# 64-wide attention on a written table of steps: values' products of a row block in one run, ten buffers for turned probabilities, blocks projected last to first

## The reference

```python
h = _rms(_layernorm(x), ln_w)
q = (h @ wq).reshape(B, S, NHEADS, HEAD_DIM)      # 32 heads of 64
k = (h @ wk).reshape(B, S, KVHEADS, HEAD_DIM)     # 8 key/value heads of 64
v = (h @ wv).reshape(B, S, KVHEADS, HEAD_DIM)
q, k = _rope(q, k)
...
scores = einsum('bqhd,bkhd->bhqk', q, k) / sqrt(HEAD_DIM)
scores = where(causal, scores, -1e30)
attn = softmax(scores, -1)
o = einsum('bhqk,bkhd->bqhd', attn, v)
x = x + o @ wo
```

## Time and profile before

| | |
|---|---|
| median of 3 runs | 2234.08 us (2233.0 to 2237.5) |
| profiled execution, its own time | 2239.73 us |
| its span in the trace | 2237.9 us |
| mean granted TensorE clock | 0.942 of full speed |
| busy share of the span | PE 86%, PEld 54%, DVE 58%, ACT 48%, POOL 40% |
| 64-wide attention, about 842 to 1869 us of the span | PE's slices at 9 tenths or more, clock at full speed in the loop |

### The profile page before, as it was taken

How to read it: one execution, slowest core, us unless ns; L and a number is a source line. 1 busy time by engine, 2 the same in 40 slices (tenths; PEclk the granted TensorE clock), 3 DMA queues, 4 the chain that set the end, 5 groups by cost and what they waited for, 6 DMA issues and landing times.

```text
span 2237.9 us, 37392 instructions
## 1 busy us (share of the span) xinstructions
PE 1923.3 (86%) x11178; PEld 1217.4 (54%) x11178; DVE 1292.1 (58%) x3257; ACT 1080.4 (48%) x2758; POOL 905.6 (40%) x1013
## 2 busy tenths in 40 slices
PE   4979899778787739999999999999999996599995
PEld 2656778533333325666666666666666665455552
DVE  5775453457568466666666666666666665822222
ACT  3324342345455416665566556656665663144442
POOL 4990000022120004444444444444444443468884
PEclk9989899769999979999999999999999997799997
DMA  4000020000000100000000000000000003545556
GB/s 143 1 1 1 9 49 1 1 1 1 1 13 26 39 2 1 1 0 0 0 0 0 0 0 0 0 0 0 0 0 0 0 0 111 206 70 82 84 83 160
DMA packets 61350, 60.76 MB, mean 27 GB/s; under 512 B 13136, under 2 KB 58320, under 8 KB 61264
## 3 DMA queue, kind: packets, MB, share of 16 engines
q0 software_dynamic: 15360, 20.98, 5.9%
q1 hardware_dynamic: 45904, 38.65, 5.4%
HBM read 40.48 MB, written 19.14 MB: 27 GB/s over the span
## 4 chain that ended last, share of the span: by engine, by line
PE 62%; DVE 14%; issue 11%; ACT 7%; POOL 4%; DMA 2%; SPq 0%; ACTq 0%; DVEq 0%; POOLq 0%
PE banks L1804 8%; PE banks L1827 7%; PE banks L1836 6%; PE banks L1815 5%; PE banks L1846 4%; PE banks L1900 3%; PE banks L2024 2%; PE banks L1858 2%; ACT wide_x L1468 2%; PE banks L1875 2%; POOL wdT L751 2%; PE banks L1649 2%; ACT wugT L1482 2%; PE banks L1920 2%; PE banks L1942 1%
## 5 line engine op out<-in xcount | busy, mean ns | idle before, releaser
L1051 DVE TENSOR_REDUCE con<-banks 128x1 f32<-128x256 f32 (+3 forms) x512 | 250.3, 489 | 147.9 <-PE banks L1806 141.1
L1804 PE MATMUL banks<-wide_k,wide_q 128*128 128x512 f32 (+3 forms) x1024 | 300.9, 376 | 0.5 <-ACT wide_k L1419 0.5
L683 POOL TENSOR_TENSOR wugT<-wugT,con 128x512 f32<-128x512 f32 (+1 forms) x256 | 237.6, 934 | 134.8 <-DVE con L1041 134.3
L1804 PEld LDWEIGHTS banks<-wide_k,wide_q 128*128 128x128 f32 x1024 | 159.4, 190 | 132.3 <-issue 87.7
L1827 PE MATMUL banks<-attn 128*64 128x256 f32 x1280 | 208.5, 404 | 0.9 <-ACT attn L1447 0.9
L1846 PE MATMUL banks<-late,xnT 128*128 (+1 forms) x512 | 197.2, 508 | 9.7 <-DVE xn L1067 6.3
L1083 DVE TENSOR_REDUCE con<-banks 128x2 f32<-128x1024 f32 x128 | 154.7, 1214 | 66.5 <-PE banks L1888 65.6
L694 POOL TENSOR_TENSOR attn<-attn 128x320 f32<-128x320 f32 x128 | 111.0, 867 | 200.3 <-DVE attn L1029 200.3
L1432 ACT ACTIVATE wugT<-banks,con 128x512 f32<-128x512 f32 (+1 forms) x256 | 161.1, 632 | 58.4 <-DVE con L1051 55.1
L1836 PE MATMUL banks<-late,attn 128*128 (+1 forms) x512 | 141.7, 399 | 28.1 <-DVE attn L1034 25.9
L2024 PE MATMUL banks<-w,late 128*128 x320 | 158.0, 617 | 2.2 <-ACT late L1561 1.7
(11 more groups left out here) (309 smaller groups left out, 4111.6 us busy)
## 6 DMA issues: line engine op xcount, KB each, us to landing
w<-in_L_ffn_w_dram SPq DMA_DIRECT2D x32, 256.0 KB, 6.4
late<-in_L_ffn_w_dram SPq DMA_DIRECT2D x16, 256.0 KB, 6.4
y_rows<-wqkv1T SPq DMA_DIRECT2D x1, 2176.0 KB, 7.9
x<-in_L_attn_x_dram SPq DMA_DIRECT2D x4, 512.0 KB, 9.1
late<-in_L_ffn_wq_dram SPq DMA_DIRECT2D x2, 1024.0 KB, 7.2
late<-in_L_ffn_wo_dram SPq DMA_DIRECT2D x1, 2048.0 KB, 8.3
h_rows<-wugT SPq DMA_DIRECT2D x1, 2048.0 KB, 7.0
y_rows<-x SPq DMA_DIRECT2D x1, 2048.0 KB, 12.8
```

The lines of the kernel that those rows point to most:

```text
L683: nc.gpsimd.tensor_tensor(p, p, rinv[:, m:m + 1].to_broadcast([P, n]), ALU.mult).then_inc(at.sem["norm"], 1)
L1051: nc.vector.tensor_reduce(negmax[:, a:a + 1], bank[at.sbank(a)][:, 0:P * at.keys(at.row_of(a))], AX, ALU.max, negate=True).then_inc(at.sem ...
L1804: nc.tensor.matmul(sbank[:, 0:keys], wide_q[:, side, i, qcols], wide_k[:, side, w, 0:keys], start=(w == 0), stop=False)
```

## The change

The worked-out list gives way to a written table `WIDE`, which is the steady list; "first", "last" and "drain" are cut from it by round. `n_turned` goes from 5 buffers to 10, one for each pair, and the two waits on the buffer are dropped. Token blocks are projected in the order 3, 2, 1, 0 (`wide_tile`), and the wait before the values copy is now for the last pair that reads that block. The values steps stand in four runs: 0 to 3, 4 to 6, 7 and 8, and 9.

```diff
-            def __init__(self, name, quads, hd, causal, bufs, n_turned, pieces, lag, behind, rest, prepare, late):
+            def __init__(self, name, quads, hd, causal, bufs, n_turned, pieces, behind, schedule):
...
-                rounds = self.stream(4)
...
+                steady = [op for slot in range(self.units) for op in [("scores", 0, slot)] + schedule.get(slot, [])]
...
-        WIDE_NEXT = {0: [("stage", 0)], 4: [("qkv", 0)], 6: [("split", 0), ("qkv", 1)], 7: [("turn_qk", 0)],
...
+        WIDE = {0: [("stage", 1, 0), ("turn", -1, 8)],
+                1: [("project", -1, 1)],
+                2: [("qkv", 1, 0), ("values", -1, 7), ("values", -1, 8)],
+                3: [("turn", -1, 9)],
+                4: [("project", -1, 2), ("split", 1, 0)],
+                5: [("values", -1, 9), ("qkv", 1, 1)],
+                6: [("turn_qk", 1, 0)],
+                7: [("project", -1, 3), ("turn_qk", 1, 1), ("turn", 0, 0), ("split", 1, 1)],
+                8: [("turn", 0, 1), ("qkv", 1, 2)],
+                9: [("turn_qk", 1, 2), ("turn", 0, 2)],
+                10: [("turn_qk", 1, 3), ("turn", 0, 3), ("split", 1, 2), ("qkv", 1, 3)],
+                11: [("turn", 0, 4)],
+                12: [("turn_qk", 1, 4), ("turn", 0, 5), ("values", 0, 0), ("values", 0, 1), ("values", 0, 2), ("values", 0, 3),
+                     ("split", 1, 3)],
+                13: [("turn_qk", 1, 5), ("turn", 0, 6)],
+                14: [("turn_qk", 1, 6), ("project", 0, 0)],
+                15: [("turn_qk", 1, 7), ("values", 0, 4), ("values", 0, 5), ("values", 0, 6), ("turn", 0, 7)]}
+
+        def wide_tile(a):
+
+            return TB - 1 - a
...
-                if t == 0 and reached(n - 1):
-                    v.wait_ge(at.sem["pv"], (n - 1) * len(at.steps))
+                if reached(n - 1):
+                    v.wait_ge(at.sem["pv"], (n - 2) * len(at.steps) + at.last_step(t) + 1)
...
-                        if reached(n0 + a + 1 - at.n_turned):
-                            act.wait_ge(at.sem["pv"], n0 + a + 1 - at.n_turned)
-                        nc.scalar.activation(at.probsT[:, a % at.n_turned, :], bank[PTBANK[1]][:],
+                        nc.scalar.activation(at.probsT[:, a, :], bank[PTBANK[1]][:],
```

More of the change, by code:

```diff
@@ L281, in two_layers @@
         wide_k = operands("wide_k", 4 * S).rearrange("p (u h n) -> p u h n", u=2, h=2)
-        region = Region(second.enter_context(nc.sbuf_tensor("attn2", [P, 5 * S + 512 + 1280 + 4 * S + 512 + DC * B * S], F32)))
-        wide_bufs = shared_buffers(5)
+        region = Region(second.enter_context(nc.sbuf_tensor("attn2", [P, 10 * S + 512 + 1280 + 4 * S + 512 + DC * B * S], F32)))
+        wide_bufs = shared_buffers(10)
         wide_x = operands("wide_x", 2 * (R64 + 2) * P).rearrange("p (u n) -> p u n", u=2)
@@ L318, in __init__ @@
                 self.steps = [(q, k) for q, (r, _g) in enumerate(quads) for k in range(self.keys(r))]
+                assert n_turned == len(self.steps)
                 self.sem = {n: sem(f"{name}_{n}") for n in self.names}
                 self.turns = TB * pieces
-                rounds = self.stream(4)
-                assert rounds[1] == rounds[2] and len(rounds) == 5
-                self.windows = {"first": [op for op in rounds[0] if (op[0], op[2]) not in sum(late.values(), [])],
-                                "steady": rounds[2], "last": [op for op in rounds[3] if op[1] <= 0], "drain": rounds[4]}
+                steady = [op for slot in range(self.units) for op in [("scores", 0, slot)] + schedule.get(slot, [])]
+                self.windows = {"first": [op for op in steady if op[1] >= 0], "steady": steady,
+                                "last": [op for op in steady if op[1] <= 0], "drain": [op for op in steady if op[1] < 0]}
                 uses = lambda w: sum(op[0] in ("qkv", "project") for op in self.windows[w])
@@ L351, in y_before @@
                 return TB if window == "first" else it * self.y_uses["per_round"] + self.y_uses["steady"]
[L353 to L390, removed]
-                    slot += 1
-                return out
         RING = 16
@@ L414, in projected_at @@
             return (n, rest // 2) if rest in (0, 2) and 0 <= n < B else None
-        WIDE_NEXT = {0: [("stage", 0)], 4: [("qkv", 0)], 6: [("split", 0), ("qkv", 1)], 7: [("turn_qk", 0)],
-                     8: [("turn_qk", 1), ("split", 1), ("qkv", 2)], 9: [("turn_qk", 2)],
-                     10: [("turn_qk", 3), ("split", 2), ("qkv", 3)], 11: [("turn_qk", 4)], 12: [("turn_qk", 5), ("split", 3)],
-                     13: [("turn_qk", 6)], 14: [("turn_qk", 7)]}
+        WIDE = {0: [("stage", 1, 0), ("turn", -1, 8)],
[17 more added lines that the diff above has]
+            return TB - 1 - a
         def prologue(pieces):
@@ L439, in two_layers @@
                                           "norm", "onT", "y_ps", "y")}
-        a2 = Attention("a2", [(r, 0) for r in reversed(range(TB))], HD64, True, wide_bufs, 5, 2, 4, 2, 5, WIDE_NEXT, {})
+        a2 = Attention("a2", [(r, 0) for r in reversed(range(TB))], HD64, True, wide_bufs, 10, 2, 2, WIDE)
         SBANK, PTBANK, OBANK, MBANK, YBANK = (0, 1, 2), (3, 4), 5, 6, 7
@@ L1068, in dve_work @@
                     elif kind == "qkv":
-                        rope(at, n, a, wide_v[:, (par + d) % 2, a, :])
+                        rope(at, n, a, wide_v[:, (par + d) % 2, wide_tile(a), :])
                     elif kind == "split":
@@ L1845, in pe_work @@
                         for c in range(DC):
-                            ins = nc.tensor.matmul(bank[YBANK][:, 0:QKV], xnT[:, c, P * a:P * a + P], w_qkv(n, c),
+                            ins = nc.tensor.matmul(bank[YBANK][:, 0:QKV], xnT[:, c, P * wide_tile(a):P * wide_tile(a) + P], w_qkv(n, c),
                                                    start=(c == 0), stop=(c == DC - 1))
```

17 lines of the change are left out of this document (6 added, 11 removed).

## The result

The changed kernel takes 2142.49 us (median of 4 runs, 2131.14 to 2144.82) against 2235.79 before: a ratio of 0.9569, 95% interval 0.9538 to 0.9599, or 93 us less. The forecast was 2129 with a range of 2095 to 2180.

The account below looks back on a forecast made before the run. PE's queue was taken to bound the kernel. Gains of 1.9 (runs), 1.3 (bank) and 0.3 (modes), less 0.2 (splits), make 3.3 us a round; 105 us in all with the ends, 2234.1 to 2129 us, range 2095 to 2180.

Parts of the forecast that it names:

- Runs: Ten single values steps become four runs on PE, saving entry and exit costs: 1.9 us a round.
- Rival 3: Column halves run in parallel inside a values run, 63 us more gained: about 2066 us, chance 0.01.
- Ten buffers: Copies of turned probabilities lose a wait met early; direct gain 0 to 0.1 us a round, taken as 0.
- Bank 7: Project and qkv spread out in this bank: waits from 1.6 to 0.3 us a round, the rest before qkv 0.
- Splits: Splits moved on ACT: waits of 0.7 us at turn_qk 6, 0.2 at turn_qk 4; split waits from 0.8 to 1.0.
- The sum: All terms of a loop round together: 3.3 us less, 99 us over thirty rounds.
- The five places: PE waits before qkv 1, project 2, turn_qk 2, project 3 and turn_qk 6 in the old kernel: 2.4 us a round.
- term for turns and scores behind a project or qkv: Turns and scores no longer follow a project or qkv in the wrong mode, at four places: 0.3 us a round.
- Outside the loop: First and last rounds merge values too, 1.5 us less each; the drain, with one projection less, 3 us less.
- Rival 1: Waits eat more, POOL slowing DVE on splits 1 to 3: only 1.6 us a round gained, 2180 us, chance 0.19.
- Rival 2: Bank and split waits both vanish, leaving PE work of 27.6 us a round: 2090 us, chance 0.10.
- Rivals 4 and 5: 4: late reduction, exponential and split delay slots 10 to 14, 2315 us, chance 0.03; 5: no change, 2230 to 2238, 0.02.

Follow-up runs that it names:

- three_moves: Changed kernel with qkv 0 behind values 7 and 8, split 2 ahead of turn 3, split 3 ahead of turn 5: 2083.1 us, 27.41 a round.
- three_single: `three_moves` with the values steps taken apart again, one to a slot: 2151.0 us, 29.57 a round.
- five_buffers: Changed kernel with five buffers for turned probabilities instead of ten, and the two buffer waits put back: 2146.2 us, 29.24 a round.
- qkv0_last: Changed kernel with qkv 0 behind values 7 and 8 in slot 2 instead of ahead of them: 2121.0 us, 28.49 a round.
- split3_first: Changed kernel with split 3 ahead of turn 5 and values 0 to 3 in slot 12: 2129.1 us, 28.73 a round.

## Why the prediction was right, and where its terms were off

**What bounds it.** PE's queue: shown. The clock in the loop stayed at full speed, no DMA came in, and with nearly all waits out (`three_moves`) the round is PE's own.

**Runs, forecast 1.9 us a round.** Right as a size: 1.82 on the old order with nearly the same waits on either side, and 1.9 between `three_single` and `three_moves`, once the few waits are taken off. The Trainium skill ("TensorEngine Tiling (Array Packing)", Key Properties) has the engine drained at a change of tiling mode; entry and exit costs of 0.25 to 0.34 us that fall on a run and not on a step agree with that. Rival 3, that page's parallel column tiles, is out: each further four matmuls take 0.43 us, 0.11 each, one after the other.

**Ten buffers, forecast 0.** Right: `five_buffers` 29.24 against 29.19.

**Bank 7, forecast 1.3 gained, with 0.3 left at qkv 0.** Mis-sized: 0.56 to 0.71 stayed there, in turn from round to round, and 0.16 before project 3. Over the loop the waits for this bank went from 1.8 us a round to 0.8, 1.0 gained. PE's own way there (946.64 to 948.10, 1.46) and DVE's sum (starting 0.17 after the project's end, lasting 0.42) were as forecast. What I left out is between the end of the wait and the first matmul. The chain of waits in the changed kernel, and then what PE's weight queue does on the qkv's lines in the same time (source L1813, the wait, and L1815):

```profile
947.89 0.43 DVE xn L1038
948.32 0.34 issue
948.66 1.55 PE banks L1815 x4
```

```profile
L1813 PEldq EVENT_SEMAPHORE  x1: 51/51/51, 948.4 to 948.4; - x1
```

```profile
L1815 PEldq FUSED_REGOPS  x2: 51/51/51, 948.6 to 948.7; - x2
L1815 PEldq ALU_OP  x1: 36/36/36, 948.5 to 948.5; - x1
```

Which layer weights qkv 0 multiplies by depends on the round's number, held in registers, and the register steps (ALU_OP, FUSED_REGOPS) stand behind the wait, so 0.34 us pass where project 2 before needed 0.05 (947.61 + 0.21 to 947.87). Qkv 1 in the kernel before is the nearest comparison: the same line and the same kind of wait, for DVE's sum, but the registers are worked out once a round, ahead of qkv 0. There it is 0.05 too, from this row of DVE's timeline (944.48 + 0.42) to 944.95:

```profile
944.48 0.42 DVE L1067 TENSOR_TENSOR xn<-xn,banks 128x256 f32 x1 [0.60 <-PE banks L1836]
```

`qkv0_last` removes wait and rest, 0.71. That the register work is the 0.3 is thus read from traces; no run took it out alone.

**Splits, forecast 0.7 at turn_qk 6 and 0.2 at turn_qk 4.** Right: 0.70 and 0.32, and both vanish when the splits stand early. Of the 0.70, 0.47 belongs to split 3's place at the end of ACT's slot 12; the rest, ACT's late copy of turn_qk 5, was in no term, and goes only if split 2 is early too.

**The sum, forecast 3.3 a round, measured 3.07.** Two counts in it were off, and nearly made up for each other, which is luck. I had put waiting before at 2.4 us a round; it was 2.8. The five places hold 0.38, 0.60, 0.36, 0.60 and 0.42, as I had them, but turn_qk 0 (0.21) and project 1 (0.19) wait too and were left out. And I had waiting after at about 1.3, where five places (turn_qk 4, turn_qk 6, qkv 0, project 3, turn_qk 3) hold 0.32 + 0.70 + 0.64 + 0.16 + 0.11 = 1.9, and the round could still fall by 1.79. So waits fell by 0.9 where 1.1 was forecast, the runs gave their 1.9, and what is left of the 3.07, 0.3, fits the term for turns and scores behind a project or qkv; that term was not tried apart. That also overturns how I split the gain: runs 1.9, order 1.4, to be added. They do not add. The runs are worth 1.82 on the old order and 0.23 on the new, the order 2.76 for single steps and 1.17 for runs (30.36 to 29.19). Each takes up slack that the other needs.

**Outside the loop.** The first round gave 2.0 more instead of 1.5 less, the last and the drain 3.4 less instead of 4.5. With 91.8 for 99 in the loop this makes 93 for 105.

**The rivals.** Rival 1 (more waits) was the nearest in kind: waits were 1.9 us a round and not 1.3. But not by its mechanism. Its price came from DVE and POOL meeting on the splits 1 to 3. In the changed kernel DVE's part of splits 1 to 3 takes 0.63 each (split 0 1.12, with POOL busy), as in this row of its DVE timeline, split 3:

```profile
940.53 0.63 DVE L1044 TENSOR_TENSOR wide_x<-attn,wide_x 128x256 fp32r<-128x256 f32 x2 [1.81 <-ACT wide_x L1437]
```

DVE idles 1.81 us ahead of it, and is busy 590 of 876 us in the loop: the order of ACT's queue makes this wait, and not DVE's load. The Trainium skill warns of copies out of PSUM ("TensorEngine Tiling (Array Packing)", PSUM Bottleneck): they are no engine's limit here, but waits for such a copy are part of what is left, 0.8 us a round for DVE to empty bank 7, and before turn_qk 3 and 6 some 0.1 and 0.2 for ACT's copies of turned operands. Split 1 at 0.63 instead of 1.19, with split 0 at 1.12 instead of 0.99, is 0.4 of the 1.4 us a round that DVE is less busy; the rest is open. Rival 2 (no waits at all, 27.6 a round, 2090 us) did not come with this table, but `three_moves` reaches it, 27.41 and 2083. Rivals 4 and 5 are excluded by the interval, though rival 4's chain (split 2, the rotary steps, the maximum of unit 11, the exponential) is there, once a round, in ACT's 2.02 us of idle time, as long in the changed kernel as in `split3_first`. PE itself nowhere waits for a score bank.

## What to carry to other kernels

When an in-order engine loses work, ask at once what that work was covering: price the runs and the order together, and walk the new order once from start to start. A step whose operands come through two other engines must be placed on those engines' queues too; here moving two splits up in ACT's order and one qkv behind a run was worth more than half of what the whole change had gained. And compare a stage by a step that recurs in it: 29.19 and 29.20 us a round in two executions whose whole times were 7 us apart.

## What the runs showed of the hardware that was not expected

- Qkv 0, with register steps of its own behind the wait, started 0.34 or 0.35 us after the operation that it waited for had ended, in each of six rounds, where steps without them started 0.05 to 0.15 after it.
- In stages that no kernel here changes, `stage` of the prologue started anywhere from 802.2 to 816.3 us in the profiled executions.
